# One input of the long two-input VectorE operations of the attention stages placed in PSUM

## The chip, the core and the metric

The kernel runs on one core of a Trainium2 chip. The metric is device time in microseconds (us) for one execution of the whole program; lower is better. The core has TensorE (PE: matmuls; its weight loads are listed apart as PEld), VectorE (DVE), ScalarE (ACT), GpSimd (POOL) and SyncE (SP), each with an instruction queue of its own. They share SBUF, the working memory, and PSUM, the memory that matmuls write. The engines wait for one another through semaphores.

## The reference

Four graph layers follow one another on 12,500 nodes and 400,000 edges, each with a residual and a layer norm. Edges are sorted by destination. Only the first layer, two rounds of graph attention, is touched by the change. One round, cut:

```python
def _gat_layer(x, src, dst, W, a_s, a_d, b, heads, outc):
    h = (x @ W).reshape(N, heads, outc)
    alpha_s = (h * a_s).sum(-1)
    alpha_d = (h * a_d).sum(-1)
    e = jax.nn.leaky_relu(alpha_s[src] + alpha_d[dst], SLOPE)
    m = jax.ops.segment_max(e, dst, num_segments=N)
    p = jnp.exp(e - m[dst])
    z = jax.ops.segment_sum(p, dst, num_segments=N)
    alpha = p / (z[dst] + 1e-16)
    out = jax.ops.segment_sum(h[src] * alpha[:, :, None], dst, num_segments=N)
    return out.reshape(N, heads * outc) + b
```

The first round has 3 heads, the second has 1. The other three layers compute a message for every edge (from products of node and edge features) and add the messages up by source or destination.

## The kernel before

The 400,000 edges lie as 128 partitions x 3125 columns. Each stage walks over them in 125 chunks of 25 columns, with two buffers in turn. Stages follow one another with a barrier between them. Those that matter here:

- **count_destinations** (called hist_d in the rows). For each chunk `OneHots.make` builds two tables of zeros and ones from the 25 keys of each partition: `hot_a` (key shifted right by 7, compared with the numbers 0 to 97, 25 x 98 = 2450 elements) and `hot_k` (key and 127, compared with 0 to 127, 25 x 128 = 3200 elements). TensorE multiplies them into a count per node.
- **attention("gat1")**, with `CountSources` as its extra work: the same tables and counts for the sources (hist_s in the rows), woven into the first attention round.
- **attention("gat2")**, with `PlaceBySource` as its extra work: the tables for 20 of the 25 columns (1960 and 2560 elements; place in the rows) and, by five groups of four columns, a chain PE, ACT, PE, DVE which finds each edge's place in the order by source.

In `attention`, GpSimd issues 25 indirect DMAs per chunk (L864): each reads 128 row numbers from the SBUF tile `gat_idx` and gathers 128 rows of the node table into `gat_got`. It may start on chunk i+1 when chunk i-1 is done (`done`) and the row numbers have come (`idx_in`). VectorE first does `ask` for a chunk (scores and running maximum, short operations on 25 to 75 elements), ScalarE takes the exponentials (L936, into the SBUF tile `gat_ex_out`), and VectorE does `weigh`: one product of the gathered features with the exponentials (L912, `gat_px`; 1200 elements in gat1, 800 in gat2), then one scan of 25 elements for each feature (L919, L922; 51 in gat1, 33 in gat2) and a copy (L924), which raises `done`. `ask` waits until all 25 gathers of its chunk have landed (L893).

All order is written out by hand. In gat1 VectorE's order for a chunk is tables, `ask`, `weigh`. In gat2 each turn of VectorE weaves the placing of the chunk before (`mask` L1067, `take` L1075 and L1077) with `ask`, `weigh` and the tables of the present one.

The comparison numbers 0 to 127 lie in SBUF as bf16, `iota_b`, and are read again for every column by a broadcast. L279 writes `hot_a`, L281 writes `hot_k`; both have two inputs in SBUF, `iota_b` and `part_b`. So has L912, `gat_got` and `gat_ex_out`.

Of the kernel before, what the change touches and what calls it, by code (L numbers as in the profile page):

```python
# [5 lines left out]
P = 128  # L6
CW = 25
# [105 lines left out]
def gnn_kernel(nc, x, src, dst, edge_attr_16, edge_attr_8, node_vec1,  # L113
# [72 lines left out]
    with root:  # L186
# [74 lines left out]
        class OneHots:  # L261


            def __init__(self, name, cols, ctx):
                self.cols = cols
                self.key = [sb(f"{name}_key{b}", [P, cols], I32, ctx) for b in range(2)]
                self.part = sb(f"{name}_part", [P, 2, cols], I32, ctx)
                self.part_b = sb(f"{name}_part_b", [P, 2, cols], BF16, ctx)
                self.hot_a = [sb(f"{name}_hot_a{b}", [P, cols, NP], BF16, ctx) for b in range(2)]
                self.hot_k = [sb(f"{name}_hot_k{b}", [P, cols, NK], BF16, ctx) for b in range(2)]  # L270

            def make(self, chain, dve, b, ready):
                chain.add(dve.tensor_scalar(self.part[:, 0, :], self.key[b][:, :], 7, None,
                                            ALU.logical_shift_right))
                chain.link(dve.tensor_scalar(self.part[:, 1, :], self.key[b][:, :], NK - 1, None,
                                             ALU.bitwise_and))
                chain.link(dve.tensor_copy(self.part_b[:, :, :], self.part[:, :, :]))
                pa, pk = (self.part_b[:, n, :].unsqueeze(2) for n in range(2))
                chain.add(dve.tensor_tensor(self.hot_a[b][:, :, :], iota_b[:, 0:NP].unsqueeze(1).to_broadcast([P, self.cols, NP]),  # L279
                                            pa.to_broadcast([P, self.cols, NP]), ALU.is_equal))  # L280
                dve.tensor_tensor(self.hot_k[b][:, :, :], iota_b[:, :].unsqueeze(1).to_broadcast([P, self.cols, NK]),  # L281
                                  pk.to_broadcast([P, self.cols, NK]), ALU.is_equal).then_inc(ready, 1)

        class Histogram:
# [18 lines left out]
            def dve_start(self, dve):  # L303
                dve.memset(self.zero[:, :], 0.0).then_inc(self.zero_set, 1)
                self.chain = Chain(dve, self.steps)

# [504 lines left out]
        def attention(name, heads, feats, table, tw, sums, last_rows, extra):  # L811
# [6 lines left out]
            with ExitStack() as ctx:  # L818
# [15 lines left out]
                    ("steps", "spread", "asked", "said", "done", "admitted", "let_in", "first_got", "start_steps"))  # L834
                extra.allocate(ctx)
                block = ctx.enter_context(nc.Block())

# [32 lines left out]
                def _(dve):  # L870
# [36 lines left out]
                    def weigh(i, b, turn, first):  # L907
# [4 lines left out]
                        ch.link(dve.tensor_tensor(px[:, :, :, :], g_x.unsqueeze(1).to_broadcast([P, heads, feats, CW]),  # L912
                                                  p.unsqueeze(2).to_broadcast([P, heads, feats, CW]), ALU.mult))
                        if not first:
# [18 lines left out]
                def _(act):  # L933
                    def exponential(i, b, turn, first):
                        act.wait_ge(asked, i + 1)
                        act.activation(ex_out[:, :, :, :], ex_in[:, :, :, :], ACT.Exp).then_inc(said, 1)  # L936

# [13 lines left out]
        class CountSources:  # L951


            def allocate(self, ctx):
                self.hist = Histogram("hist_s", src_v, True, ctx)

            def sync(self, sp, i, b, turn, first):
# [31 lines left out]
        class PlaceBySource:  # L989
# [5 lines left out]
            def allocate(self, ctx):  # L995
                self.groups = [list(range(t, min(t + LANES, CP))) for t in range(0, CP, LANES)]
                self.G = len(self.groups)
                ps = lambda n: ctx.enter_context(nc.psum_tensor(n, [P, 512], F32))
                self.hots = OneHots("place", CP, ctx)
                self.loaded = [sem(f"place_loaded{b}") for b in range(2)]  # L1000
# [16 lines left out]
                     "copied", "placed"))  # L1017

            def sync(self, sp, i, b, turn, first):
                if not first:  # L1020
                    sp.wait_ge(self.ready, i - 1)
                sp.dma_start(self.hots.key[b][:, :], src_v[:, bass.ds(i * CW, CP)]).then_inc(self.loaded[b], 16)

            def sync_end(self, sp):
                pass

            def vector_start(self, dve):
                self.chain, self.late_chain = Chain(dve, self.steps), Chain(dve, self.late_steps)

            def make_hots(self, dve, i, b, turn, first):  # L1030
                self.chain.begin(i)
                dve.wait_ge(self.loaded[b], 16 * turn + 16)
                if not first:
                    dve.wait_ge(self.counted, self.G * (i - 1) + 1)
                    dve.wait_ge(self.placed, i - 1)
                self.hots.make(self.chain, dve, b, self.ready)

# [32 lines left out]
            def take(self, dve, ch, i, b, g):  # L1070
# [4 lines left out]
                ch.link(dve.tensor_tensor(self.tmp[:, 0:n, :], self.look_ps[q][:, 0:n * NK].rearrange("p (t k) -> p t k", k=NK),  # L1075
                                          self.hots.hot_k[b][:, ts[0]:ts[0] + n, :], ALU.mult))
                dve.tensor_reduce(self.place[b][:, ts[0]:ts[0] + n], self.tmp[:, 0:n, :], AX_X, ALU.add).then_inc(self.summed, 1)  # L1077
# [45 lines left out]
            def tensor(self, pe, i, b, turn, first):  # L1123
                G = len(self.groups)
                hot_a, hot_k = self.hots.hot_a[b], self.hots.hot_k[b]

# [979 lines left out]
```

## Time and profile before

| what | us |
|---|---|
| median of 3 runs (lowest, highest) | 28349.22 (28346.67, 28424.53) |
| span of the profiled execution | 34032.4 |
| count_destinations, in that span | about 0.04 to 0.86 ms |
| attention gat1, 125 chunks | 1.27 to 6.03 ms |
| attention gat2, 125 chunks | 6.65 to 12.63 ms |
| all that follows | 12.63 to 34.03 ms |

The profiled execution took 34032.4 us, a fifth longer than the runs that were timed without a profile. The page gives, over its span: PE busy 50%, DVE 50%, ACT 11%, POOL 57%. The rows below are in microseconds from the span's start, durations marked ns in nanoseconds. In a timeline row the bracket holds the idle time of the engine before the instruction and what ended it; "issue" means that the profile shows nothing that it waited for, "remote" that the semaphore was raised at a time that fits none of the recorded instructions. The end of a matmul is modelled, not recorded.

### The profile page before, as it was taken

To read this page: it belongs to the slowest core of one execution; us is meant where nothing else is said; L and a number is where in the kernel's file an instruction comes from. 1 tells how busy PE (TensorE), PEld (TensorE's weight loads), DVE (VectorE), ACT (ScalarE), POOL (GpSimd) and SP (SyncE) were. 2 spreads that over 40 slices of the span, in tenths; PEclk is the share of its full clock that TensorE was granted. 3 is DMA by queue.
4 is the path that set the end of the run, shared out by engine and by line. 5 is a ranking of instruction groups with operands and counts; after the bars stand their busy time and mean duration, and the time that the engine had idled before them with its cause. 6 is when DMAs were issued, how large, how long until landed. Compare 5 with 4: busy or idle time off the path is not lost. (4 is left out here: it accounts for less than half of the span.)

```text
span 34032.4 us, 315667 instructions
## 1 busy us (share of the span) xinstructions
PE 16860.3 (50%) x98808; PEld 12028.2 (35%) x98808; DVE 17082.3 (50%) x40576; ACT 3681.0 (11%) x7157; POOL 19447.1 (57%) x17570
## 2 busy tenths in 40 slices
PE   4100000244444435777744666666666627666663
PEld 3100000133333333555532333333333325555552
DVE  9355555155555543555533444444444536555654
ACT  0000000111111111111100111111111001111110
POOL 0677777655555554666625555555555555555554
PEclk6555555555555556888856777777777757777776
DMA  3011111011111110000010000000000110000001
GB/s 125 19 27 27 27 27 27 15 21 21 21 21 20 20 19 13 22 22 22 21 53 14 13 14 14 14 14 14 14 14 14 27 42 17 17 18 18 17 17 58
DMA packets 1032557, 815.73 MB, mean 24 GB/s; under 512 B 602134, under 2 KB 922910, under 8 KB 1028512
## 3 DMA queue, kind: packets, MB, share of 16 engines
q0 software_dynamic: 561792, 189.30, 5.0%
q1 hardware_dynamic: 366264, 291.81, 3.3%
q10 hardware_dynamic: 104400, 333.49, 2.5%
q8 instruction: 38, 0.62, 0.0%
q14 instruction: 63, 0.52, 0.0%
HBM read 416.39 MB, written 396.80 MB: 24 GB/s over the span
## 5 line engine op out<-in xcount | busy, mean ns | idle before, releaser
L864 POOL DMA_INDIRECT gat_got<-table,gat_idx x6250 | 7051.8, 1128 | 3590.9 <-issue 2742.8
L1335 POOL DMA_INDIRECT msgs<-msg_msg,msg_pos x4875 | 6040.2, 1239 | 3732.2 <-DVE msg_msg L2055 1716.9
L1245 PE MATMUL sheaf_dps<-sheaf_dhotq,sheaf_dleft 128*128 128x392 bf16 x18000 | 3743.5, 353 | 2039.7 <-issue 2038.6
L1245 PE MATMUL msg_dps<-msg_dhotq,msg_dleft 128*128 128x392 bf16 x16500 | 3613.5, 372 | 354.9 <-issue 353.7
L1553 POOL DMA_INDIRECT msgs<-sheaf_msg,sheaf_pos x1625 | 1759.8, 1083 | 3362.5 <-issue 3362.5
L1545 POOL DMA_INDIRECT sheaf_got<-table,sheaf_idx x3125 | 2967.5, 950 | 953.0 <-issue 952.0
L1159 PE MATMUL place_look_ps<-place_nexts,place_hot_at 98*128 98x128 f32 x5000 | 1659.9, 473 | 3073.7 <-ACT place_nexts L1101 1741.3
L1245 PEld LDWEIGHTS sheaf_dps<-sheaf_dhotq,sheaf_dleft 128*128 128x128 bf16 x18000 | 1821.4, 102 | 3707.7 <-issue 2736.9
L327 PE MATMUL hist_s_counts<-hist_s_hot_k,hist_s_hot_a 128*98 128x128 bf16 x3125 | 362.8, 314 | 4362.2 <-DVE hist_s_hot_k L281 4362.2
L1159 PEld LDWEIGHTS place_look_ps<-place_nexts,place_hot_at 98*128 98x128 f32 x5000 | 1320.8, 324 | 3322.3 <-issue 2329.0
L1600 DVE TENSOR_TENSOR sheaf_v<-sheaf_vps,b_pair 128x800 f32<-128x800 f32 x125 | 124.0, 992 | 4586.7 <-PE sheaf_vps L1660 4542.2
L1245 PEld LDWEIGHTS msg_dps<-msg_dhotq,msg_dleft 128*128 128x128 bf16 x16500 | 1805.3, 115 | 1737.9 <-issue 1021.8
L1402 PE MATMUL msg_mps<-w_edge,msg_flip 128*128 128x16 f32 x12500 | 1663.2, 267 | 1257.5 <-issue 1256.2
L1427 ACT COPY msg_flip<-msg_fps 128x512 f32<-128x512 f32 x2625 | 1340.4, 541 | 8065.6 <-PE msg_fps L1386 3567.3
L1402 PEld LDWEIGHTS msg_mps<-w_edge,msg_flip 128*128 128x128 f32 x12500 | 1717.7, 212 | 1250.3 <-issue 1249.6
L1372 DVE TENSOR_TENSOR msg_outer<-msg_att,msg_own 128x6400 f32<-128x6400 f32 x125 | 1700.8, 13607 | 462.8 <-remote 438.4
L1363 DVE TENSOR_TENSOR_SCAN msg_own<-keep_d,msg_own,msg_ex 128x25 f32<-128x25 f32 x6000 | 1121.2, 257 | 1537.8 <-DMA msg_ex<-ex 1172.1
L327 PEld LDWEIGHTS hist_s_counts<-hist_s_hot_k,hist_s_hot_a 128*98 128x98 bf16 x3125 | 336.5, 203 | 4389.1 <-DVE hist_s_hot_k L281 4389.1
L1386 PE MATMUL msg_fps<-ident,msg_outer 128*128 128x128 f32 x9375 | 1534.6, 296 | 592.8 <-issue 509.1
L919 DVE TENSOR_TENSOR_SCAN gat_acc<-gat_ex_out,gat_acc,gat_px 128x25 f32<-128x25 f32 x10000 | 1697.7, 247 | 185.8 <-issue 175.9
L1386 PEld LDWEIGHTS msg_fps<-ident,msg_outer 128*128 128x128 f32 x9375 | 1247.6, 156 | 830.9 <-issue 612.9
L1660 PE MATMUL sheaf_vps<-w_pair,sheaf_hid 128*128 128x32 f32 x6250 | 860.5, 281 | 950.8 <-ACT sheaf_hid L1687 602.3
(459 smaller groups left out, 27121.6 us busy)
## 6 DMA issues: line engine op xcount, KB each, us to landing
gat_got<-table,gat_idx POOLq DMA_INDIRECT x6250
msg_ex<-ex SPq DMA_DIRECT2D x250, 400.0 KB
gat_sums<-gat_acc ACTq DMA_DIRECT2D x125, 675.0 KB
msgs<-msg_msg,msg_pos POOLq DMA_INDIRECT x4875
tail_m<-msgs SPq DMA_DIRECT2D x75, 800.0 KB
src_sums<-tail_acc ACTq DMA_DIRECT2D x75, 800.0 KB
gat_sums<-gat_acc ACTq DMA_DIRECT2D x125, 425.0 KB
ex<-zeros ACTq DMA_DIRECT2D x25, 2000.0 KB
```

The costliest lines, as they stand in the source:

```text
L864: pool.indirect_dma_start(got[b][:, j, :], None, table, bass.IndirectOffsetOnAxis(idx[b][:, j:j + 1], 0)).then_inc(gathered[b], 16)
L919: dve.tensor_tensor_scan(acc[b][:, :, c], ex_out[:, 0, h, :], px[:, h, f, :], acc[1 - b][:, CW - 1, c:c + 1], ALU.mult, ALU.add)
L1159: pe.matmul(self.look_ps[q][:, n * NK:(n + 1) * NK], self.hot_at[g][:, n, :], self.nexts[q][:, n, :], start=True, stop=False, skip_group_c ...
L1245: last = pe.matmul(self.acc[:, n, 0:self.BQ], left[:, s_, t, :], hot_q[:, t, n * self.BQ:(n + 1) * self.BQ], start=False, stop=False, skip ...
L1335: pool.indirect_dma_start(msgs, bass.IndirectOffsetOnAxis(pos[b][:, j:j + 1], 0), msg[b][:, j, :], None).then_inc(scattered[b], 16)
L1363: last = dve.tensor_tensor_scan(own[b][:, f, :], kp, ex[b][:, :, f], own[1 - b][:, f, CW - 1:CW], ALU.mult, ALU.add)
L1372: dve.tensor_tensor(outer[b][:, :, :].rearrange("p t (l r) -> p t l r", r=ra), left.unsqueeze(3).to_broadcast([P, CW, la, ra]), right.unsq ...
L1386: last = pe.transpose(flip_ps[(b * U + u) % 2][:, k * P:(k + 1) * P], outer[b][:, t, n * P:(n + 1) * P], ident[:, :])
L1402: last = pe.matmul(msg_ps[b][:, t * D:(t + 1) * D], flip[q][n][:, k * P:(k + 1) * P], weights[n], start=(n == 0), stop=(n == lots - 1), sk ...
L1427: act.copy(flip[q][n][:, 0:len(ts) * P], flip_ps[(b * U + u) % 2][:, 0:len(ts) * P]).then_inc(copied, 1)
L1545: pool.indirect_dma_start(got[b][:, j, :], None, table3, bass.IndirectOffsetOnAxis(idx[b][:, j:j + 1], 0)).then_inc(gathered[b], 16)
L1553: pool.indirect_dma_start(msgs_2, bass.IndirectOffsetOnAxis(pos[b][:, j:j + 1], 0), msg[b][:, j, :], None).then_inc(scattered[b], 16)
```

## The change

A class `OneHots` now also owns one PSUM bank, `aside`, of 512 fp32 values per partition. Its first 128 hold the comparison numbers as fp32, copied there once per stage by VectorE (`start`); the tables are made from these and from `part_b`, which stays in SBUF. Behind them lies room for the exponentials of the product, `p_ps` (75 values per partition in gat1, 25 in gat2). ScalarE writes the exponentials a second time, to `p_ps`, and raises `said` after that one; L912 reads them there, and `gat_got` stays in SBUF. The scans go on reading `gat_ex_out` in SBUF. The rest of the diff renames `hots` to `one_hots` in `PlaceBySource`.

```diff
@@ class OneHots
                 self.key = [sb(f"{name}_key{b}", [P, cols], I32, ctx) for b in range(2)]
+                self.aside = ctx.enter_context(nc.psum_tensor(f"{name}_aside", [P, 512], F32))
+                self.numbers = self.aside[:, 0:NK]
+                self.numbered = sem(f"{name}_numbered")
...
+            def start(self, dve):
+                dve.tensor_copy(self.numbers, iota_b[:, :]).then_inc(self.numbered, 1)
+                dve.wait_ge(self.numbered, 1)
...
-                chain.add(dve.tensor_tensor(self.hot_a[b][:, :, :], iota_b[:, 0:NP].unsqueeze(1).to_broadcast([P, self.cols, NP]),
+                chain.add(dve.tensor_tensor(self.hot_a[b][:, :, :], self.numbers[:, 0:NP].unsqueeze(1).to_broadcast([P, self.cols, NP]),
                                             pa.to_broadcast([P, self.cols, NP]), ALU.is_equal))
-                dve.tensor_tensor(self.hot_k[b][:, :, :], iota_b[:, :].unsqueeze(1).to_broadcast([P, self.cols, NK]),
+                dve.tensor_tensor(self.hot_k[b][:, :, :], self.numbers.unsqueeze(1).to_broadcast([P, self.cols, NK]),
                                   pk.to_broadcast([P, self.cols, NK]), ALU.is_equal).then_inc(ready, 1)
@@ class Histogram
                 dve.memset(self.zero[:, :], 0.0).then_inc(self.zero_set, 1)
+                self.hots.start(dve)
@@ def attention
+                p_ps = extra.hots().aside[:, NK:NK + heads * CW].rearrange("p (h t) -> p h t", t=CW)
...
                         ch.link(dve.tensor_tensor(px[:, :, :, :], g_x.unsqueeze(1).to_broadcast([P, heads, feats, CW]),
-                                                  p.unsqueeze(2).to_broadcast([P, heads, feats, CW]), ALU.mult))
+                                                  p_ps.unsqueeze(2).to_broadcast([P, heads, feats, CW]), ALU.mult))
...
                         act.wait_ge(asked, i + 1)
-                        act.activation(ex_out[:, :, :, :], ex_in[:, :, :, :], ACT.Exp).then_inc(said, 1)
+                        act.activation(ex_out[:, :, :, :], ex_in[:, :, :, :], ACT.Exp)
+                        act.activation(p_ps, ex_in[:, 1, :, :], ACT.Exp).then_inc(said, 1)
@@ class PlaceBySource
             def vector_start(self, dve):
+                self.one_hots.start(dve)
```

The one instruction that is added per chunk stands in ScalarE's queue. Its first chunks in gat1, before (each row: its place, line, operation, output and inputs, size of the output):

```order
29 L936 ACTIVATE gat_ex_out<-gat_ex_in 128x150
30 L940 DMA gat_sums<-gat_acc 128x1350
31 L936 ACTIVATE gat_ex_out<-gat_ex_in 128x150
32 L940 DMA gat_sums<-gat_acc 128x1350
```

and in the changed kernel, where `hist_s_aside` is the PSUM bank of gat1:

```order
29 L945 ACTIVATE gat_ex_out<-gat_ex_in 128x150
30 L946 ACTIVATE hist_s_aside<-gat_ex_in 128x75
31 L950 DMA gat_sums<-gat_acc 128x1350
32 L945 ACTIVATE gat_ex_out<-gat_ex_in 128x150
33 L946 ACTIVATE hist_s_aside<-gat_ex_in 128x75
34 L950 DMA gat_sums<-gat_acc 128x1350
```

Between the exponentials and the store of the sums there is now a second, half as large, pass of exponentials. On VectorE, in the first chunk of gat1 of the changed kernel, the operations stand as before but for one copy ahead of all, and three of them name the bank as an input:

```order
144 L276 CAST hist_s_aside<-iota_b 128x128
145 L280 TENSOR_SCALAR hist_s_part<-hist_s_key 128x25
146 L282 TENSOR_SCALAR hist_s_part<-hist_s_key 128x25
147 L284 CAST hist_s_part_b<-hist_s_part 128x50
148 L286 TENSOR_TENSOR hist_s_hot_a<-hist_s_aside,hist_s_part_b 128x2450
149 L288 TENSOR_TENSOR hist_s_hot_k<-hist_s_aside,hist_s_part_b 128x3200
...
158 L921 TENSOR_TENSOR gat_px<-gat_got,hist_s_aside 128x1200
```

No operation changed its place among the others, on this engine or on any other.

## Rows read from the trace of the kernel before

**Rows 1.** Busy time by stretch: length, busy us of each engine (instructions), clock, DMA.

```profile
40.00:860.00 820.00, 359.86 (x3108) 332.90 (x3109) 809.47 (x626) 0.00 (x0) 0.00 (x0) 0.60 0.33 129
1268.00:6030.00 4762.00, 363.91 (x3127) 336.77 (x3127) 2522.18 (x8768) 41.02 (x125) 3739.41 (x3126) 0.52 0.14 27
6653.00:12630.00 5977.00, 2539.09 (x15002) 2189.26 (x15000) 3005.84 (x8004) 1024.61 (x2000) 3313.59 (x3126) 0.52 0.12 21
```

**Rows 2.** GpSimd's gathers, gat1 then gat2: duration ns min/median/max, then idle by cause.

```profile
L864 POOL DMA_INDIRECT gat_got<-table,gat_idx x3125: 938/944/3473, 1270.1 to 6009.1; - x196
...
L864 POOL DMA_INDIRECT gat_got<-table,gat_idx x3125: 938/944/2756, 6655.0 to 12553.9; - x196
  issue: 1753.9, 3063
  DVE gat_acc L924: 825.4, 60
```

**Rows 3.** Timeline of gat1, GpSimd: start, us, engine, what [idle before].

```profile
3059.35 0.98 POOL L864 DMA_INDIRECT gat_got<-table,gat_idx  x1 [0.30 <-issue]
3060.64 0.94 POOL L864 DMA_INDIRECT gat_got<-table,gat_idx  x1 [0.30 <-issue]
3061.89 3.28 POOL L864 DMA_INDIRECT gat_got<-table,gat_idx  x1 [0.30 <-issue]
3065.47 3.10 POOL L864 DMA_INDIRECT gat_got<-table,gat_idx  x1 [0.30 <-issue]
...
3088.84 1.93 POOL L864 DMA_INDIRECT gat_got<-table,gat_idx  x1 [0.30 <-issue]
```

**Rows 4.** Timeline of the same stretch, VectorE.

```profile
3059.90 0.24 DVE L919 TENSOR_TENSOR_SCAN gat_acc<-gat_ex_out,gat_acc,gat_px 128x25 f32<-128x25 f32 x1
...
3061.63 2.71 DVE L279 TENSOR_TENSOR hist_s_hot_a<-iota_b,hist_s_part_b 128x2450 bf16<-128x2450 bf16 x1
3064.26 3.48 DVE L281 TENSOR_TENSOR hist_s_hot_k<-iota_b,hist_s_part_b 128x3200 bf16<-128x3200 bf16 x1
...
3085.05 0.24 DVE L893 COPY gat_top<-gat_top 128x3 f32<-128x3 f32 x1 [16.78 <-DMA gat_got<-table,gat_idx]
...
3087.57 2.43 DVE L912 TENSOR_TENSOR gat_px<-gat_got,gat_ex_out 128x1200 f32<-128x1200 f32 x1 [0.40 <-issue]
```

**Rows 5.** Timeline of gat2: a table, then a product with one input in PSUM.

```profile
9002.40 2.82 DVE L281 TENSOR_TENSOR place_hot_k<-iota_b,place_part_b 128x2560 bf16<-128x2560 bf16 x1
9003.61 2.42 POOL L864 DMA_INDIRECT gat_got<-table,gat_idx  x1 [0.30 <-issue]
...
9007.27 0.68 DVE L1075 TENSOR_TENSOR place_tmp<-place_look_ps,place_hot_k 128x512 f32<-128x512 f32 x1
9007.59 0.94 POOL L864 DMA_INDIRECT gat_got<-table,gat_idx  x1 [0.30 <-issue]
```

**Rows 6.** Timeline of a later stage: two SBUF inputs, then one, beside scatters.

```profile
14018.72 3.49 DVE L1372 TENSOR_TENSOR msg_outer<-msg_own,msg_att 128x3200 f32<-128x3200 f32 x1
14019.55 3.51 POOL L1335 DMA_INDIRECT msgs<-msg_msg,msg_pos  x1 [0.30 <-issue]
...
14026.45 2.65 DVE L1934 RECIPROCAL msg_work<-msg_work 128x400 f32<-128x400 f32 x1
14027.17 0.97 POOL L1335 DMA_INDIRECT msgs<-msg_msg,msg_pos  x1 [0.30 <-issue]
```

**Rows 7.** Timeline of gat2, waits of GpSimd and VectorE.

```profile
9023.03 0.61 PE L1140 MATMUL place_same_ps<-place_hot_at_b 98*128 98x128 bf16 x4 [1.72 <-ACT place_hot_at L1090]
9026.05 0.69 DVE L1067 TENSOR_TENSOR place_same<-place_same_ps,earlier 128x512 bf16<-128x512 f32 x1 [8.46 <-remote]
9046.00 0.94 POOL L864 DMA_INDIRECT gat_got<-table,gat_idx  x1 [13.75 <-issue]
```

**Rows 8.** Groups of gat1 and gat2 by line, busy us, mean ns.

```profile
L936 ACT ACTIVATE gat_ex_out<-gat_ex_in 128x150 f32<-128x150 f32 x125 | 41.0, 328 | 4727.5 <-issue 3607.8 <-DVE gat_ex_in L904 1119.7
L912 DVE TENSOR_TENSOR gat_px<-gat_got,gat_ex_out 128x800 f32<-128x800 f32 x125 | 197.4, 1579 | 0.3 <-issue 0.3
```

More of the change, by code:

```diff
@@ L955, in allocate, with hots @@
                 self.hist = Histogram("hist_s", src_v, True, ctx)
+            def hots(self):
+                return self.hist.hots
             def sync(self, sp, i, b, turn, first):
@@ L998, in allocate @@
                 ps = lambda n: ctx.enter_context(nc.psum_tensor(n, [P, 512], F32))
-                self.hots = OneHots("place", CP, ctx)
+                self.one_hots = OneHots("place", CP, ctx)
                 self.loaded = [sem(f"place_loaded{b}") for b in range(2)]
@@ L1017, in allocate, with hots @@
                      "copied", "placed"))
+            def hots(self):
+                return self.one_hots
             def sync(self, sp, i, b, turn, first):
@@ L1021, in sync @@
                     sp.wait_ge(self.ready, i - 1)
-                sp.dma_start(self.hots.key[b][:, :], src_v[:, bass.ds(i * CW, CP)]).then_inc(self.loaded[b], 16)
+                sp.dma_start(self.one_hots.key[b][:, :], src_v[:, bass.ds(i * CW, CP)]).then_inc(self.loaded[b], 16)
             def sync_end(self, sp):
@@ L1035, in make_hots @@
                     dve.wait_ge(self.placed, i - 1)
-                self.hots.make(self.chain, dve, b, self.ready)
+                self.one_hots.make(self.chain, dve, b, self.ready)
             def vector(self, dve, now, before, ask, weigh):
@@ L1075, in take @@
                 ch.link(dve.tensor_tensor(self.tmp[:, 0:n, :], self.look_ps[q][:, 0:n * NK].rearrange("p (t k) -> p t k", k=NK),
-                                          self.hots.hot_k[b][:, ts[0]:ts[0] + n, :], ALU.mult))
+                                          self.one_hots.hot_k[b][:, ts[0]:ts[0] + n, :], ALU.mult))
                 dve.tensor_reduce(self.place[b][:, ts[0]:ts[0] + n], self.tmp[:, 0:n, :], AX_X, ALU.add).then_inc(self.summed, 1)
@@ L1124, in tensor @@
                 G = len(self.groups)
-                hot_a, hot_k = self.hots.hot_a[b], self.hots.hot_k[b]
+                hot_a, hot_k = self.one_hots.hot_a[b], self.one_hots.hot_k[b]
                 def turn_(g):
```

## The prediction

> **What bounds the kernel now.** I read the busy time by stretch first. In count_destinations VectorE is busy for 809.47 of 820 us: that stage is VectorE's alone, and GpSimd has no work in it [rows 1]. In gat1 GpSimd is busy for 3739.41 of 4762 us with 3126 DMA instructions, VectorE for 2522.18. Next the gathers themselves: their median is 944 ns, but single ones take up to 3473 [rows 2]. The timeline shows what stands between two of them: 0.30 us, always, so that an undisturbed gather starts every 1.25 us (3060.64 to 3061.89) [rows 3]. 25 x 1.25 = 31.2 us of a chunk of 4762 / 125 = 38.1 us is that cadence. At the end of `ask`'s first scans VectorE waits 16.78 us for the gathers [rows 4]. So gat1 is bound by GpSimd, with next to no idle time on it beyond the 0.30 us.
>
> The remaining time is in the long gathers. 3126 at 944 ns would be 2951 us; the busy time is 3739, so 788 us, 6.3 us per chunk, are excess [rows 1, 2]. The timeline says which they are: the gather at 3061.89 takes 3.28 us and the one at 3065.47 takes 3.10 [rows 3], and VectorE's two tables run at 3061.63 for 2.71 us and at 3064.26 for 3.48 [rows 4]; the third, 1.93 us, lies beside L912, 2.43 us. Each long gather ends some 0.8 to 0.9 us after the VectorE operation that it lay beside ended: it waited and then did its normal work.
>
> Is it the length of the operation, or its inputs? In gat2 a gather beside L1075 (one input in PSUM, one in SBUF, 0.68 us) takes 0.94, while the one beside L281 (two SBUF inputs, 2.82 us) takes 2.42 [rows 5]. In a later stage a scatter beside a product of two SBUF inputs takes 3.51 us, and one that starts inside a reciprocal with one input, 2.65 us long, takes 0.97 [rows 6]. Length alone doesn't block; two long SBUF inputs do.
>
> The Trainium skill says the same in "SBUF — State Buffer", section "SBUF: two separate sides": VectorE and GpSimd share a port pair that is held for a whole instruction, by a VectorE operation with two SBUF inputs only against a GpSimd instruction that reads SBUF. The trace agrees, 3.51 against 0.97 us. By that rule all three operations would stop blocking.
>
> gat2 looks different. GpSimd is busy for 3313.59 of 5977 us [rows 1] and idles 13.75 us ahead of each chunk [rows 7], 1753.9 + 825.4 us in all [rows 2]. In the profiled execution it waits for `done`, late because the placing is late. But this placing waits for releases that the recorded work doesn't account for: the matmuls of L1140 end by 9023.64, yet VectorE's L1067 that needs them starts at 9026.05 after 8.46 us of idleness, released "remote" [rows 7]. And the profiled execution is 5683 us longer than the median of the runs without a profile (34032.4 against 28349.22). I take it that a good part of these waits is the profiler's: TensorE's many small matmuls leave the most records, and gat1 has few of them (3127 against 15002 [rows 1]). Without these waits GpSimd would need 25 x 1.25 + 2.9 + 0.3 = 34.4 us per chunk in gat2 (2.9 is its excess, (3313.59 - 3126 x 0.944) / 125), and VectorE's busy time is 24.0, PE's 20.3, ACT's 8.2. I expect gat2 to be bound by GpSimd too when no profile is taken, at about 35 us, where the profile shows 47.8.
>
> **The change, part by part.**
>
> Tables in count_destinations: 250 operations, VectorE's alone. Their rate now: (3.48 - 2.82) us / (3200 - 2560) elements = 1.03 ns per element, and 0.18 us fixed [rows 4, 5]. By this a product of 512 elements would take 0.71 us; L1075, with one input in PSUM, takes 0.68 [rows 5]. So a PSUM input costs nothing: 0 us. That row reads PSUM once, straight through; the tables read the same 128 numbers again and again, as fp32 beside bf16, which no row shows. Bounds: -10 us, and, were the input taken at half the rate, 5650 x 1.03 ns x 125 = +730 us. I take 0, since L1075 has the very mixture of fp32 from PSUM and bf16 from SBUF.
>
> gat1: the three long operations of a chunk stop blocking. Of the 788 us some stay: a gather beside the scans takes 0.98 us, 0.04 more, and their inputs don't move [rows 3, 4]. The 51 scans of a chunk, of 0.24 us and overlapping, fill at most 12 us, 6 to 9 gathers: some 30 us in all stay. That leaves -760 us, all on the path, as GpSimd has no slack. If L912 is not freed (its SBUF input comes first and its PSUM input second, the reverse of L1075, and no row shows that form) the gain is less by 0.99 us per chunk by [rows 3], at most 1.9: -120 to -240 us. What is late next: VectorE's wait of 16.78 us shrinks by 6.3 to some 10 us and stays positive, so GpSimd bounds gat1 afterwards too, at 31.8 us per chunk.
>
> gat2: the two tables free 2.9 us per chunk, 363 us. L912 with 800 elements takes 1.58 us [rows 8]; in the profile it falls into GpSimd's idle time, without a profile it would block for half of itself or so, 0.8 us, 100 us in all (bounds 0 and 1.58 us). Together -460 us if GpSimd alone set the pace before and after. Afterwards it needs 31.5 us, and the chain of mask, look-up, take and `weigh` over PE, ACT and VectorE comes close: VectorE 24.0 us busy, plus two or three turnarounds of 1.7 to 3 us where it has nothing else to do. I take -400 us; bounds 0 (the chain bound it anyway, as in the profile) and -520.
>
> ScalarE: one more activation per chunk, 75 or 25 elements. The present one, 150 elements, takes 0.33 us [rows 8]; the second adds 0.2 to 0.3 us ahead of `said`, in VectorE's path from `ask` to L912. Who waits: L912 and, 14 us later, `done`. In gat1 VectorE's spare 10 us hide it; without that cover it would cost 0.3 x 125 = 38 us. In gat2 VectorE does a take and a mask between `ask` and `weigh`, 2 us, which hides it; behind it on ScalarE stand the copies for the second group, for which TensorE waits. That is inside my 60 us of discount. The copy of the numbers and its wait stand three times in the program: under 1 us.
>
> Sum on the profiled execution: -760 us in gat1, about 0 in gat2, since there GpSimd idles anyway: span about 33,270. Sum for the timed runs: 0 - 760 - 400 = -1160, from 28349 to **27190 us**.
>
> **Rivals.**
>
> (1) gat2 is not bound by GpSimd even without a profile. For it: 13.75 us of idle per chunk in the only trace there is [rows 7]. Against it: the fifth by which profiling stretches the program must lie somewhere. Time: 28349 - 760 = 27590.
>
> (2) L912 goes on blocking since its first input is in SBUF. For it: no row has this form. Against it: it has one SBUF input only, like the reciprocal [rows 6]. Time: 27190 + 240 + 100 = 27530.
>
> (3) The change doesn't do what it seems to: the block depends on something else than the memory of the inputs, on the written amount perhaps (tables write 3200 elements, L1075 only 512). Against it: the reciprocal writes 400 in 2.65 us and does not block, while a product of 25 elements already costs 0.04 [rows 3, 4, 6]. Time: 28350.
>
> (4) Slower: the PSUM input is slow when it is read by a broadcast. Place: the tables, in all three stages. In count_destinations every added ns per element costs 5650 x 125 = 706 us. In gat1 it costs nothing until VectorE's 20.2 us of busy time grow to 31; in gat2 it takes the gain away from about +1 ns. It decides from +1.1 ns per element, twice the present price: 780 us lost against 760 won. At three times the price (+2.06 ns): +1450 in count_destinations, +11.6 us per chunk in gat1 (VectorE at 32 plus its waits, the gain is gone), +9 us in gat2, some +500: about 30,300.
>
> The Trainium skill has a rule that points this way, in "VectorE: DVE Perf Modes", section "Why PSUM operands drop a tier": with an operand in PSUM the fastest modes are closed, and fp32 is held to one element per cycle. Were 1.03 ns per element a faster mode's rate, the tables would come to twice the price: the +730 us of my bound, and 27920 at the most favourable. But the product of 512 elements with a PSUM input has that same rate by the row, so no tier is lost by it.
>
> **How the numbers follow.** My forecast, 27190: 0.52. Rival 1, 27590: 0.25. Rival 2, 27530: 0.08. Rival 3, 28350: 0.05. Rival 4, above 28,500: 0.04. The last 0.06 is for more gain than I count, down to 26,900: a GpSimd that is never held may also meet fewer late `done`s (4762 - 3739 us in gat1 are 85 us more than 3126 x 0.30, and these are not in my sum). A range of 27,000 to 27,700 holds the first three cases with their bounds, 0.8 or more. Within 0.3% means 85 us, about what a measurement of this kernel can tell from no change. Faster by more: 0.91; within: 0.05; slower by more: 0.04.
>
> **What would show it.** In the profile after: no gather in gat1 or gat2 much over 1 us (the maximum of 3473 ns gone to about 1100); GpSimd's busy time in gat1 near 2980 us; gat1 some 4000 us long; tables at 2.71 and 3.48 us as before and count_destinations still 820 us. Gathers of 2 us and more beside L912 alone would be rival 2, beside all three rival 3. A longer table is rival 4. GpSimd's idle time ahead of each chunk of gat2 would grow in the profile from 13.75 to about 17 us. If the timed gain is near 760 us, the gain in gat2 was the profiler's time and mine was a wrong guess about what the waits there are.

## The result, and the profile after

| | us |
|---|---|
| before, median of 4 timed runs | 28350.85 (28346.67 to 28424.53) |
| after, median of 4 timed runs | 27113.65 (27099.84 to 27162.9) |
| after, the profiled execution's span | 27161.2 |
| ratio of the runs, with its 95% interval | 0.9565 [0.955, 0.9579] |

The change takes 1237 us away, a little more than the 1160 of the forecast. The profiled execution is one of the four, and the slowest of them (27162.9 us). First the busy time by stretch of the kernel after: count_destinations, gat1, gat2, with the columns of [rows 1].

```profile
40.00:860.00 820.00, 359.97 (x3117) 333.04 (x3118) 808.56 (x627) 0.00 (x0) 0.00 (x0) 0.59 0.33 129
1243.00:5206.00 3963.00, 363.91 (x3127) 336.77 (x3127) 2482.77 (x8759) 56.56 (x250) 2994.13 (x3125) 0.52 0.16 32
5834.00:9790.00 3956.00, 2462.57 (x14897) 2150.73 (x14896) 2991.07 (x7989) 1001.18 (x2115) 2974.24 (x3126) 0.53 0.16 31
```

count_destinations has not moved. gat1 is 3963 us long, and GpSimd's busy time in it is 2994.13 for the same 3125 gathers. VectorE's busy time is nearly the same as in [rows 1]: nothing became cheaper on VectorE. What went away is time in which GpSimd's instructions had waited.

The gathers of the kernel after by themselves, gat1 and then gat2 (duration ns min/median/max; GpSimd's idle time by cause, us and times; who waited for them), as [rows 2] had them:

```profile
L873 POOL DMA_INDIRECT gat_got<-table,gat_idx x3125: 940/947/1098, 1244.4 to 5189.9; - x196
...
  issue: 952.3, 3124
...
  DVE gat_top L902: 1323.3, 125
...
L873 POOL DMA_INDIRECT gat_got<-table,gat_idx x3125: 941/947/1017, 5836.1 to 9761.3; - x196
...
  issue: 952.4, 3124
...
  DVE gat_top L902: 488.4, 125
```

The longest gather has gone from 3473 ns to 1098, the median has not moved. The idle time is 0.30 us times 3124 and nothing else, in both stages: GpSimd runs gather after gather from the first to the last. VectorE waits for it in every chunk, 1323.3 / 125 = 10.6 us in gat1 and 488.4 / 125 = 3.9 us in gat2.

The timeline of the kernel after in gat1, VectorE (start, us, engine, what), where [rows 4] stood:

```profile
3044.81 0.17 DVE L902 COPY gat_top<-gat_top 128x3 f32<-128x3 f32 x1 [10.59 <-DMA gat_got<-table,gat_idx]
...
3047.38 2.41 DVE L921 TENSOR_TENSOR gat_px<-gat_got,hist_s_aside 128x1200 f32<-128x1200 f32 x1 [0.52 <-ACT hist_s_aside L946]
...
3059.45 2.71 DVE L286 TENSOR_TENSOR hist_s_hot_a<-hist_s_aside,hist_s_part_b 128x2450 bf16<-128x2450 f32 x1
3062.08 3.48 DVE L288 TENSOR_TENSOR hist_s_hot_k<-hist_s_aside,hist_s_part_b 128x3200 bf16<-128x3200 f32 x1
```

And GpSimd beside the product and beside the tables:

```profile
3047.56 0.95 POOL L873 DMA_INDIRECT gat_got<-table,gat_idx  x1 [0.30 <-issue]
3048.82 0.95 POOL L873 DMA_INDIRECT gat_got<-table,gat_idx  x1 [0.30 <-issue]
...
3052.60 0.98 POOL L873 DMA_INDIRECT gat_got<-table,gat_idx  x1 [0.30 <-issue]
...
3060.32 0.94 POOL L873 DMA_INDIRECT gat_got<-table,gat_idx  x1 [0.30 <-issue]
3061.56 0.95 POOL L873 DMA_INDIRECT gat_got<-table,gat_idx  x1 [0.30 <-issue]
```

The tables take 2.71 and 3.48 us as in [rows 4], to the digit, and the product 2.41 for 2.43. The gathers in the middle of them take 0.94 and 0.95 us, where they took 3.28, 3.10 and 1.93 [rows 3]. Beside the scans (3052.60), whose inputs all still lie in SBUF, a gather takes 0.98, as before.

### The profile page after: what moved, and what is told of

Read it like the earlier page. It is cut to its first block and busy times, and to the rows that moved or that the text cites. A ratio compares the mean times of both kernels' runs of the same rounds, so it can differ in the third digit from the quotient of the medians.

```text
span 27161.2 us, 315919 instructions
## 1 busy us (share of the span) xinstructions
PE 16179.7 (60%) x98805; PEld 12079.2 (44%) x98808; DVE 16979.6 (63%) x40579; ACT 3692.9 (14%) x7407; POOL 19454.9 (72%) x17570
## 5 line engine op out<-in xcount | busy, mean ns | idle before, releaser
L1352 POOL DMA_INDIRECT msgs<-msg_msg,msg_pos x4875 | 6814.5, 1398 | 1566.6 <-issue 1449.1
L873 POOL DMA_INDIRECT gat_got<-table,gat_idx x6250 | 5967.9, 955 | 1909.1 <-issue 1904.8
L1562 POOL DMA_INDIRECT sheaf_got<-table,sheaf_idx x3125 | 3245.9, 1039 | 953.3 <-issue 952.5
L1262 PE MATMUL sheaf_dps<-sheaf_dhotq,sheaf_dleft 128*128 128x392 bf16 x18000 | 3312.7, 342 | 0.7 <-DVE sheaf_dhotq L1247 0.7
L1262 PE MATMUL msg_dps<-msg_dhotq,msg_dleft 128*128 128x392 bf16 x16500 | 3282.7, 354 | 0.0
L1403 PE MATMUL msg_fps<-ident,msg_outer 128*128 128x128 f32 x9375 | 1699.7, 332 | 1471.7 <-DVE msg_outer L1389 1471.7
L1403 PEld LDWEIGHTS msg_fps<-ident,msg_outer 128*128 128x128 f32 x9375 | 1428.2, 176 | 1701.1 <-issue 1522.8
L1419 PEld LDWEIGHTS msg_mps<-w_edge,msg_flip 128*128 128x128 f32 x12500 | 1591.7, 207 | 0.0
L1419 PE MATMUL msg_mps<-w_edge,msg_flip 128*128 128x16 f32 x12500 | 1573.1, 269 | 0.0
L1654 PE MATMUL sheaf_cps<-ident,sheaf_cat 128*32 128x128 f32 x3125 | 602.7, 321 | 1051.5 <-DVE sheaf_cat L1597 1051.5
```

Source lines behind the costliest of these rows:

```text
L873: pool.indirect_dma_start(got[b][:, j, :], None, table, bass.IndirectOffsetOnAxis(idx[b][:, j:j + 1], 0)).then_inc(gathered[b], 16)
L1262: last = pe.matmul(self.acc[:, n, 0:self.BQ], left[:, s_, t, :], hot_q[:, t, n * self.BQ:(n + 1) * self.BQ], start=False, stop=False, skip ...
L1352: pool.indirect_dma_start(msgs, bass.IndirectOffsetOnAxis(pos[b][:, j:j + 1], 0), msg[b][:, j, :], None).then_inc(scattered[b], 16)
L1403: last = pe.transpose(flip_ps[(b * U + u) % 2][:, k * P:(k + 1) * P], outer[b][:, t, n * P:(n + 1) * P], ident[:, :])
L1419: last = pe.matmul(msg_ps[b][:, t * D:(t + 1) * D], flip[q][n][:, k * P:(k + 1) * P], weights[n], start=(n == 0), stop=(n == lots - 1), sk ...
L1562: pool.indirect_dma_start(got[b][:, j, :], None, table3, bass.IndirectOffsetOnAxis(idx[b][:, j:j + 1], 0)).then_inc(gathered[b], 16)
```

## The experiments

The kernel before was timed on each of the chips beside these kernels, as its time differs by some 60 us from chip to chip: 28410.35 us beside the two halves, the aside in SBUF and the pieces in SBUF, 28346.67 beside the next four, 28408.24 beside the two with memsets. Ratios and gains are against these.

### The waits of gat2, and what the profile before had in it

The kernel before was profiled once more.

> The kernel before, unchanged, profiled once more. Theory (the waits of 13.75 us in gat2 of the first profile belonged to that execution, not to the kernel): a span near 28,400 us, gat1 at 37.6 and gat2 at 35.4 us per chunk, GpSimd without idle time ahead of its chunks in both. Rival: gat2 at 47 us per chunk again.

Measured: 28323.1 us with a profile, span 28321.4, beside a median of 28346.67 (7 runs), as expected. Its gathers in gat2:

```profile
L864 POOL DMA_INDIRECT gat_got<-table,gat_idx x3125: 940/944/2762, 6555.9 to 10936.6; - x196
...
  issue: 952.0, 3124
```

The idle time is 3124 times 0.30 us; what was 1753.9 + 825.4 us in [rows 2] is 952.0. The start of the stage to the start of the last gather is 4380.7 us for 3125 gathers, 35.0 us a chunk; the rival's 47 are not there. The execution on which the rows ahead of the prediction rest was a disturbed one: 34032 us where the others take 28350, longer also in stages of which the change touches nothing (msg3, the last message stage, was 5674 us long in it, and is 4798 in the kernel after). What disturbed it, no run shows. Its waits before each chunk of gat2 were that execution's, and gat2 of the kernel before is GpSimd's. Where stages of the kernel before are compared from here on, it is by this second profile.

In it, gathers beside VectorE's long operations look thus (VectorE first, then GpSimd, of one chunk of gat2):

```profile
7999.48 2.26 DVE L279 TENSOR_TENSOR place_hot_a<-iota_b,place_part_b 128x1960 bf16<-128x1960 bf16 x1
8001.67 2.81 DVE L281 TENSOR_TENSOR place_hot_k<-iota_b,place_part_b 128x2560 bf16<-128x2560 bf16 x1
...
8024.02 1.58 DVE L912 TENSOR_TENSOR gat_px<-gat_got,gat_ex_out 128x800 f32<-128x800 f32 x1
```

```profile
8000.76 1.80 POOL L864 DMA_INDIRECT gat_got<-table,gat_idx  x1 [0.30 <-issue]
8002.86 2.43 POOL L864 DMA_INDIRECT gat_got<-table,gat_idx  x1 [0.30 <-issue]
...
8024.35 2.03 POOL L864 DMA_INDIRECT gat_got<-table,gat_idx  x1 [0.30 <-issue]
```

0.86, 1.49 and 1.09 us over the undisturbed 0.94: the product does block in gat2, as the prediction had guessed without a row. What a chunk takes on GpSimd (25 times the mean distance of two gathers' starts) is 37.33 us in gat1 and 35.06 in gat2; in the kernel after 31.57 and 31.41.

### Is it the memory of the input?

```diff
-                self.aside = ctx.enter_context(nc.psum_tensor(f"{name}_aside", [P, 512], F32))
+                self.aside = sb(f"{name}_aside", [P, 512], F32, ctx)
```

> The changed kernel, with its bank aside (the comparison numbers as fp32, the second exponentials) allocated in SBUF instead of PSUM; all else, the second pass of exponentials included, as in the changed kernel. Theory (only the memory of the one input counts): the three long operations block GpSimd's gathers again, 2.2 to 2.5 us each, and the time goes back to that of the kernel before, 28,350 us within 60. Rival (the gain came from the other data type, or from the new order of waits): it stays near 27,110 us.

Measured: 28405.9 us, ratio to before 0.9999 [0.9989, 1.0008]. The same instructions, the same types and counts, and the whole gain is gone: it is as slow as the kernel before on the same chip (28410.35), and 56 us above the 28,350 that was expected from another chip. The timeline in gat1, VectorE and then GpSimd:

```profile
3064.11 2.71 DVE L286 TENSOR_TENSOR hist_s_hot_a<-hist_s_aside,hist_s_part_b 128x2450 bf16<-128x2450 f32 x1
3066.74 3.48 DVE L288 TENSOR_TENSOR hist_s_hot_k<-hist_s_aside,hist_s_part_b 128x3200 bf16<-128x3200 f32 x1
```

```profile
3064.73 2.91 POOL L873 DMA_INDIRECT gat_got<-table,gat_idx  x1 [0.30 <-issue]
3067.95 3.09 POOL L873 DMA_INDIRECT gat_got<-table,gat_idx  x1 [0.30 <-issue]
```

VectorE takes 2.71 and 3.48 us with the numbers in either memory; the gather takes 2.91 and 3.09 us with them in SBUF and 0.94 with them in PSUM. That settles two of the rivals: it is the memory, and the PSUM input costs VectorE nothing in a broadcast of fp32 beside bf16.

### Each half alone

Tables in the new form and product in the old:

```diff
-                                                  p_ps.unsqueeze(2).to_broadcast([P, heads, feats, CW]), ALU.mult))
+                                                  p.unsqueeze(2).to_broadcast([P, heads, feats, CW]), ALU.mult))
...
-                        act.activation(ex_out[:, :, :, :], ex_in[:, :, :, :], ACT.Exp)
-                        act.activation(p_ps, ex_in[:, 1, :, :], ACT.Exp).then_inc(said, 1)
+                        act.activation(ex_out[:, :, :, :], ex_in[:, :, :, :], ACT.Exp).then_inc(said, 1)
```

> The changed kernel, but the product L912 reads the exponentials from SBUF and there is no second pass of exponentials; the tables alone have an input in PSUM. Theory: a gather beside the product takes 2.5 to 3 us again, once per chunk in gat1 (up to 1.9 us more) and once in gat2 (0.8 us more): 27,110 + 240 + 100 = 27,450 us. Rival (GpSimd's losses aren't additive; one block hides another): less than 27,250 us, or above 27,700.

And the reverse, the tables' numbers read from `iota_b` again:

```diff
-                chain.add(dve.tensor_tensor(self.hot_a[b][:, :, :], self.numbers[:, 0:NP].unsqueeze(1).to_broadcast([P, self.cols, NP]),
+                chain.add(dve.tensor_tensor(self.hot_a[b][:, :, :], iota_b[:, 0:NP].unsqueeze(1).to_broadcast([P, self.cols, NP]),
...
-                dve.tensor_tensor(self.hot_k[b][:, :, :], self.numbers.unsqueeze(1).to_broadcast([P, self.cols, NK]),
+                dve.tensor_tensor(self.hot_k[b][:, :, :], iota_b[:, :].unsqueeze(1).to_broadcast([P, self.cols, NK]),
```

> The changed kernel, but the tables compare with iota_b in SBUF again; the product L912 alone reads PSUM, as its second input. Theory: the gathers beside the two tables are blocked as before, 4.2 us per chunk in gat1 and 2.9 in gat2: 27,110 + 525 + 363 = 28,000 us, and no gather beside the product is long. Rival: with the product freed, the tables block no less but at other moments, so that nothing or all is lost: above 28,250 or below 27,750 us.

| | ratio to before | gain, us | gat1, us per chunk | gat2, us per chunk |
|---|---|---|---|---|
| tables only | 0.9678 [0.9662, 0.9694] | 914.5 | 33.47 | 32.33 |
| product only | 0.9846 [0.983, 0.9863] | 436.7 | 35.29 | 34.26 |
| both | 0.9565 [0.955, 0.9579] | 1237 | 31.57 | 31.41 |

The times are 27495.82 us (27,450 expected) and 27973.61 us (28,000 expected).

With the product alone, VectorE's product and the gather that starts inside it:

```profile
3046.95 2.42 DVE L921 TENSOR_TENSOR gat_px<-gat_got,hist_s_aside 128x1200 f32<-128x1200 f32 x1 [0.52 <-ACT hist_s_aside L946]
```

```profile
3047.14 0.95 POOL L873 DMA_INDIRECT gat_got<-table,gat_idx  x1 [0.31 <-issue]
```

So a first input in SBUF and a second in PSUM frees GpSimd as well: the rival in which L912 goes on blocking is out. The halves' gains add up to 1351 us, 114 more than both together. But each half is held against the kernel before on their chip, which is 60 us slower there than beside the change (28410.35 for 28350.85), and the sum has these 60 us twice. In the profiles, against the second one of before, the tables alone take 3.86 and 2.73 us off a chunk of gat1 and gat2 and the product alone 2.04 and 0.80: 9.43 us in all, and both together 5.76 + 3.65 = 9.41. So the blocks add up here, and none hides another. The change itself was not timed on the halves' chip.

### Another way to let GpSimd in: shorter operations, all in SBUF

The kernel before, with each table in five operations of five columns and the product in four.

```diff
-                dve.tensor_tensor(self.hot_k[b][:, :, :], iota_b[:, :].unsqueeze(1).to_broadcast([P, self.cols, NK]),
-                                  pk.to_broadcast([P, self.cols, NK]), ALU.is_equal).then_inc(ready, 1)
+                for c in range(0, self.cols, 5):
+                    last = dve.tensor_tensor(self.hot_k[b][:, c:c + 5, :], iota_b[:, :].unsqueeze(1).to_broadcast([P, 5, NK]),
+                                             pk[:, c:c + 5, :].to_broadcast([P, 5, NK]), ALU.is_equal)
+                last.then_inc(ready, 1)
```

> The kernel before, all inputs in SBUF, but each table is made by operations of 5 columns (5 for 25 columns, 4 for 20) and the product by 4 operations of a quarter of the features. Theory (the block lasts for one VectorE instruction, and GpSimd gets in between two): a gather waits 0.3 to 0.4 us beside a piece of 0.6 to 0.8 us, some 2.3 us per chunk in gat1 and 1.6 in gat2 instead of 6.3 and 3.7, and VectorE's own stage grows by 8 x 0.08 us x 125 = 80 us: 27,700 us. Rival (what counts is the time that VectorE spends with two SBUF inputs, however cut): 28,350 us or more.

Measured: 27560.27 us, ratio 0.9701 [0.9685, 0.9717], 850 us better than before and 447 worse than the change (which ran on another chip). That is 140 us better than expected. VectorE's tables, and GpSimd beside them:

```profile
3052.38 3.03 DVE L280 TENSOR_TENSOR hist_s_hot_a<-iota_b,hist_s_part_b 128x490 bf16<-128x490 bf16 x5
3055.33 3.75 DVE L284 TENSOR_TENSOR hist_s_hot_k<-iota_b,hist_s_part_b 128x640 bf16<-128x640 bf16 x5
```

```profile
3053.64 1.43 POOL L868 DMA_INDIRECT gat_got<-table,gat_idx  x1 [0.30 <-issue]
3055.38 1.59 POOL L868 DMA_INDIRECT gat_got<-table,gat_idx  x1 [0.30 <-issue]
3057.27 1.17 POOL L868 DMA_INDIRECT gat_got<-table,gat_idx  x1 [0.30 <-issue]
3058.74 1.16 POOL L868 DMA_INDIRECT gat_got<-table,gat_idx  x1 [0.30 <-issue]
```

A gather now waits for no more than the rest of a piece of 0.66 or 0.82 us (it takes 0.2 to 0.7 us over 0.94; the longest of all took 1.60), and VectorE pays 0.3 us for five starts in place of one: 2.71 to 3.03. Where VectorE is the bound, that is a loss: count_destinations goes from 814 to 882 us, from the start of its first table to that of its last. The PSUM input has neither cost.

### What stood behind GpSimd in gat2

The forecast took 60 us off gat2 because the chain of mask, look-up and take came close. This kernel has 15 gathers per chunk in gat2 for 25 (so it leaves part of the work out):

```diff
-                        for j in range(CW):
+                        for j in range(GJ):
                             pool.indirect_dma_start(got[b][:, j, :], None, table,
```

> The changed kernel with 15 instead of 25 gathers per chunk in gat2 (the features of the other 10 columns are left out and read as zeros): how far was the chain over VectorE, PE and ACT from being the bound of gat2, which is 31.4 us per chunk now? Theory by the new profile, where VectorE waits 3.9 us per chunk for the gathers: 27.5 us per chunk, 27,110 - 490 = 26,620 us. Rival by the prediction (this chain needs 30 us or more): 26,930 us or more.

Measured: 26725.07 us (2 runs), ratio 0.943 [0.9411, 0.9449]: 105 us above the theory and 205 below the rival. Its gathers in gat2:

```profile
L874 POOL DMA_INDIRECT gat_got<-table,gat_idx x1875: 938/944/991, 5823.5 to 9305.7; - x188
...
  issue: 1132.7, 1813
  DVE gat_acc L937: 580.0, 60
```

Now GpSimd does wait for VectorE's copy behind the last scans: 580.0 us ahead of 60 chunks, and as long, 9.3 to 10.0 us each, ahead of nearly all the others, where the profile calls it "issue". So here the other chain sets the pace, with (9305.7 - 5823.5) / 125 = 27.9 us a chunk, 3.5 less than GpSimd's 31.4 in the kernel after. It took no part of the gain.

### The same block in a later stage

msg1 and msg3 are the message stages of the second and of the last layer. In both one VectorE product of two SBUF inputs (L1372 in [rows 6]) is VectorE's longest operation, 3.5 us in msg1 and 13.5 us in msg3, and GpSimd scatters beside it. In the kernel after, a scatter there takes up to 14200 ns against a median of 972. The stage's own tensors take 2 + 2 + 4 PSUM banks, as many as gat2 takes with its aside; an input of this product in PSUM was not tried. Instead the product was cut, into `s_` columns an operation:

```diff
+                        s_ = 5 if lots > 1 else CW
+                        for c in range(0, CW, s_):
+                            last = dve.tensor_tensor(out_4[:, c:c + s_, :, :],
```

> The changed kernel, and in the last message stage (msg3) the product of two SBUF inputs that takes 13.5 us per chunk (6400 elements, 25 columns) is made by 5 operations of 5 columns. Its chunk lasts 38.3 us with 20 scatters, one of which takes 13.8 us. Theory (the block lasts for one VectorE instruction and GpSimd's scatters set the pace there): with each piece of 2.7 us one scatter passes, 7 us of block remain instead of 12.9, so 5 to 5.6 us less per chunk: 27,110 - 650 = 26,450 us. Rival (that stage is bound by its matmuls or its loads, and the scatter merely fills in): 27,110 us, within 60.

Measured: 26700.28 us, ratio 0.9427 [0.9411, 0.9443]: 413 us better than the kernel after, where I had expected 660. Most pieces of 2.8 us let one scatter in, which then takes 2.4 us or so. But in 42 of the 125 chunks one scatter took over 5 us, the longest 14487 ns, and in 40 of these it ended only behind the last of the five pieces. And with `s_ = 1 if lots > 1 else 5`:

> As outer_5, but 25 operations of one column in msg3 and 5 of five columns in the other message stage (msg1, product of 3.5 us). Theory: pieces of 0.6 us cost a scatter 0.1 to 0.25 us each; msg3's GpSimd time falls to some 28 us per chunk and TensorE, busy for 29.8 us of 38, becomes the bound at 31 us: 7 us less per chunk, and 1 to 1.5 us in the other: 27,110 - 875 - 150 = 26,080 us. Rival (25 operations cost VectorE more than the block cost GpSimd, so that nothing is gained over 5): 26,400 us or more.

Measured: 26419.93 us, ratio 0.932 [0.9305, 0.9336]. msg1 lost 262 us (3424 to 3162), more than the theory's 150. But the time is 340 us above the 26,080 expected, since msg3 stayed at 4392 us, against 4402 with five pieces and 4798 with one. The timeline of msg3 with 25 pieces, VectorE and then GpSimd, shows why:

```profile
24034.75 15.22 DVE L1392 TENSOR_TENSOR msg_outer<-msg_att,msg_own 128x256 f32<-128x256 f32 x25
```

```profile
24034.96 1.35 POOL L1352 DMA_INDIRECT msgs<-msg_msg,msg_pos  x1 [0.30 <-issue]
24036.62 0.96 POOL L1352 DMA_INDIRECT msgs<-msg_msg,msg_pos  x1 [0.30 <-issue]
24037.88 1.50 POOL L1352 DMA_INDIRECT msgs<-msg_msg,msg_pos  x1 [0.30 <-issue]
24039.69 11.13 POOL L1352 DMA_INDIRECT msgs<-msg_msg,msg_pos  x1 [0.30 <-issue]
```

Three scatters get in between the pieces of this chunk. The fourth starts at 24039.69 and ends at 24050.82, 0.85 us after the last piece: the piece just begun and 16 more went by without letting it in. In 84 of the 125 chunks one scatter took over 5 us, and each of the 84 ended 0.84 to 0.87 us after the last piece: once left out, a scatter stays out to the end of the row of pieces. Four of the pieces by themselves:

```profile
24042.70 2.47 DVE L1392 TENSOR_TENSOR msg_outer<-msg_att,msg_own 128x256 f32<-128x256 f32 x4
```

Four pieces, each recorded as 0.67 us, span 2.47: each next piece begins 0.60 us after the last, 0.07 us before that has ended. The records show no moment without a two-input operation. That alone can't be the reason: the pieces of the tables above overlap in the same way (0.66 us, one every 0.59), and they let GpSimd in each time. Two more kernels put a memset of one column ahead of every piece but the first, one with 25 pieces and one with five:

```diff
+                            if lots > 1 and c:
+                                dve.memset(gap[:, c:c + 1], 0.0)
                             last = dve.tensor_tensor(out_4[:, c:c + s_, :, :],
```

> The kernel with 25 one-column pieces of msg3's product, with a memset of one column (128x1, into a scratch tile that nothing reads) put ahead of each piece but the first. In the run with plain pieces one scatter still took 11.13 us: it began 20 ns after a piece had begun, and 17 more pieces passed before it ended; there each piece began 599 ns after the last and was recorded as 674 ns long, so the next piece had begun before the last had ended. Theory: the scatter reads its positions only in a moment in which no operation with two SBUF inputs is under way, and back-to-back pieces leave none; an instruction without such inputs between them gives one. Then no scatter beside the pieces takes over 1.7 us, VectorE loses some 0.1 us for each of the 24 memsets (2.4 us a chunk), and msg3 goes from 35.1 us a chunk to 30 to 33, as GpSimd needs 20 x 1.27 = 25 us and VectorE 27 + 2.4: time about 26,050 us. Rival: what holds the scatter is something else (the length of the whole row of pieces, or a read by TensorE); scatters of 10 us and more stay, and the memsets only cost: 26,420 to 26,750 us.

> The kernel with msg3's product in five pieces of five columns (2.8 us each), and a one-column memset ahead of each piece but the first; msg1 in five pieces as in the kernel with 25. Theory: each memset lets one scatter through, so that no scatter beside the pieces takes over 3.7 us (two pieces' ends missed: none), where plain pieces had some of 5.2 and up to 14.5 us. Five pieces let five scatters through in 13.5 us, as most chunks did without the memsets, so the gain over plain pieces is small: msg3 about 34.5 us a chunk against 35.2, time 26,420 - 60 = 26,360 us. Rival: the memsets change nothing, scatters over 5 us stay, 26,430 us or a little more.

| | us | ratio to before | msg3, us | longest scatter in msg3, ns |
|---|---|---|---|---|
| after (one operation) | 27113.65 | 0.9565 | 4798 | 14200 |
| five pieces | 26700.28 | 0.9427 | 4402 | 14487 |
| 25 pieces | 26419.93 | 0.932 | 4392 | 15273 |
| five pieces with memsets | 26313.06 | 0.9265 [0.925, 0.928] | 4238 | 5984 |
| 25 pieces with memsets | 25842.4 | 0.9098 [0.9083, 0.9114] | 3765 | 1522 |

(From the third row on, msg1 has five pieces too, worth 262 us.) The kernel with 25 pieces and memsets, VectorE and GpSimd in msg3:

```profile
24003.38 0.76 DVE L1395 TENSOR_TENSOR msg_outer<-msg_att,msg_own 128x256 f32<-128x256 f32 x1
24003.40 0.06 DVE L1394 MEMSET msg_gap<- 128x1 f32 x1
24004.07 0.68 DVE L1395 TENSOR_TENSOR msg_outer<-msg_att,msg_own 128x256 f32<-128x256 f32 x1
24004.09 0.06 DVE L1394 MEMSET msg_gap<- 128x1 f32 x1
24004.68 0.74 DVE L1395 TENSOR_TENSOR msg_outer<-msg_att,msg_own 128x256 f32<-128x256 f32 x1
```

```profile
24003.40 0.97 POOL L1353 DMA_INDIRECT msgs<-msg_msg,msg_pos  x1 [0.31 <-issue]
24004.67 0.97 POOL L1353 DMA_INDIRECT msgs<-msg_msg,msg_pos  x1 [0.30 <-issue]
```

The scatters get through in 0.97 us, in the very stretch in which one had waited 10; the longest of the stage took 1.52, where the theory allowed 1.7. The memsets cost next to nothing, as they run beside the pieces: from piece to piece it is 0.6 to 0.7 us. And msg3 has a new bound, to be seen in its busy time by stretch, first with plain pieces, then with memsets:

```profile
21562.00:25954.00 4392.00, 3686.14 (x25920) 3087.27 (x25920) 3565.80 (x9307) 874.20 (x1736) 3590.01 (x2459) 0.84 0.09 22
...
21608.00:25373.00 3765.00, 3524.56 (x25922) 2957.45 (x25923) 3627.82 (x12308) 867.15 (x1736) 2512.68 (x2460) 0.91 0.10 26
```

GpSimd's busy time falls from 3590.01 to 2512.68 us, and VectorE is busy for 3627.82 of 3765 (TensorE, whose ends are modelled, for 3524.56); GpSimd now waits for VectorE's messages (L2079) for 547.0 us, where it had 91.4. TensorE's granted clock rises from 0.84 to 0.91 of full speed at the same time; how much of the gain is that I did not separate. Both expectations hold: 26313 for 26,360 us with five pieces, and 25842 for 26,050 with 25. With five pieces the theory's strict form fails: one scatter of the stage still took 5984 ns, so a memset between pieces makes it likely that GpSimd gets in, not certain.

The kernel with 25 pieces and memsets is the fastest of these: 9.0% under before, and 1271 us under the kernel after, although its chip is the slower one for the kernel before (28408.24 for 28350.85).

## Why the prediction was right

- **What bounds gat1.** GpSimd without slack, its excess being waits for VectorE's two-input operations: right. Its busy time came down to 2994.13 us (forecast near 2980), the chunk to 31.57 us (31.8). VectorE's wait for the gathers was to shrink from 16.78 to some 10 us: 10.59.
- **gat1, -760.** Measured between the second profile of before and after, from the stage's first to its last table, 4646 to 3932 us: -714; against the kernel with the aside in SBUF, 4681: -749. Right in mechanism, 46 us too much against the second profile. Of these some 26 are excess that only the disturbed execution had (GpSimd's busy time in gat1 is 3713.50 us in the second profile, 3739.41 in the first), and 14 that 44 us of excess stayed where 30 were forecast.
- **The waits of gat2.** That they were not the kernel's was right and carried the forecast; the argument from the profiled execution being a fifth too long was sound. The reason given, the mass of TensorE's records, was not: a second profile with the same records shows none of these waits. That this guess came out right for another reason is luck. With it fall two lines of "what would show it": a span of some 33,270 and an idle time of 17 us ahead of each chunk. In the profile after that idle time is 0.30 us.
- **gat2, -400.** This term was mis-sized. From the first to the last table 4398 to 3942 us is -456; against the kernel with the aside in SBUF, 4434, it is -492. The -460 that the prediction had before its discount was the better figure. Its parts were near: by GpSimd's busy time with each half alone, the tables' blocks cost 2.85 us a chunk (2.9 forecast) and the product's 0.92 (0.8 guessed). The discount of 60 us was the error: it put the other chain "close" to 31.5 us, from VectorE's busy 24.0 plus turnarounds; the runs with fewer gathers put it at 27.9.
- **The PSUM input costs nothing.** 2.71 and 3.48 us before and after, and 808.56 against 809.47 us in count_destinations. It held for the broadcast too, which no row had shown. The rule of the Trainium skill ("VectorE: DVE Perf Modes", section "Why PSUM operands drop a tier") that PSUM closes the fast modes had nothing to take here: the same tables with two bf16 inputs in SBUF ran no faster.
- **ScalarE's second pass.** 0.2 us (L946 has a mean of 218 ns), of which VectorE's product sees 0.12: it waits 0.52 us where it waited 0.40 [rows 4]. Hidden in gat1 by the 10.59 us, as said.
- **The rivals.** Chain-bound gat2: out by the second profile and by the fewer gathers. L912 still blocking: out by the product alone. Something other than the memory: out by the aside in SBUF. A slow PSUM broadcast: out by the tables' durations.

The sum came out 77 us short of the measured gain. Between the two profiled executions the gain is 28321.4 - 27161.2 = 1160.2 us, the forecast to the digit, and that is luck twice: gat1 gave 46 less than forecast and gat2 56 more, and the profiled execution of before (28323.1) is 28 us under the median of 28350.85, that of after (27162.9) 49 above the median of 27113.65.

## What to carry to other kernels

A long VectorE operation with two SBUF inputs holds off GpSimd's indirect transfers to its end (3.1 us for 0.95 beside the longer table), and where GpSimd sets the pace that wait is on the path however idle VectorE is; its sign is a gather whose maximum is several times its median. Put one input in PSUM, or, where that has no room, cut the operation and put a tiny instruction without two SBUF inputs between the pieces, since pieces alone may not let GpSimd in. Before a wait in a profile becomes a term of a sum, hold the profiled execution against the timed ones: where it is a fifth longer, it can't be taken at its word.

## What the runs showed of the hardware

- A row of two-input operations back to back can hold GpSimd like one: a scatter waited through 17 pieces of 0.67 us, at a spacing of 0.60; with a memset of 0.06 us ahead of each piece scatters took 0.97 us there. My expectations for five and for 25 plain pieces had missed it. The Trainium skill's "SBUF — State Buffer", section "SBUF: two separate sides", tells of a hold for a whole instruction; here it went on across instructions.
- In msg1, with five pieces of 640 elements of its product and no memsets, no scatter beside them lost more than 0.65 us, nor did any gather beside the five pieces of the tables (at most 1.60 us for 0.94). Why these rows let GpSimd in each time, while msg3's rows of five and of 25 shut it out in 42 and 84 of 125 chunks, is not settled.
- A blocked transfer has nearly all of its work still to do when the block ends: it ends 0.81 to 0.83 us behind a table, 0.75 to 0.79 behind the product of the attention stages and 0.84 to 0.88 behind msg3's, where it takes 0.94 to 0.97 undisturbed. So it is held off within its first 0.2 us.
